# Attention score steps over two units at once and V in plain float32, in a fused scan, attention and expert kernel

## The chip, the cores and the metric

One core of one Trainium2 chip. The metric is the device time of one execution in microseconds; the median of several is compared. The engines are TensorE (PE in the profile; its weight loads PEld), VectorE (DVE), ScalarE (ACT), GpSimd (POOL) and SyncE (SP, which only issues DMAs). Each works through its own list of instructions in order and waits on semaphores.

## What is computed

Eight sequences (batches) of 512 rows by 128, all float32, go through four residual blocks:

```
x = x + scan_block(layernorm(x))
x = x + experts(layernorm(x))
x = x + attention(layernorm(x))
x = x + experts(layernorm(x))
```

The attention has 16 heads of dimension 8 and a local mask: row i sees its own chunk of 10 rows and 25 rows before it.

```
q = (x @ Wq.T + bq) * 8 ** -0.5;  k = x @ Wk.T + bk;  v = x @ Wv.T + bv     # split in 16 heads
out = softmax(q @ k.T + mask) @ v;  out = out @ Wo.T + bo
```

The experts are eight dense feed-forward nets of width 512 (silu(x Wg) * (x Wu), then Wd), each weighed row by row by a product of two softmaxes. The scan block is a gated state space recurrence with 8 states for each of 64 channels.

## The kernel before

**Passes and chunks.** The main work is the experts: two for each batch, 16 passes (ORDER, line 33) of 32 chunks, 512 chunks in all. A chunk c on TensorE is the gate product pg (three float32r products of 512 columns, `split3`, lines 286 to 289), the up product pu of chunk c - 1, and the down products pd of chunk c - 4 (line 1123; 0, 8 or 16 records a chunk, in a pattern of four chunks). A plain float32 product runs as two records. Pass 0 does halves of two batches side by side. ACT turns pg into h by silu (line 1183), DVE multiplies h by pu (line 1232) and every fourth chunk adds the weighed pd to x (line 1220). TensorE may start the gate product of chunk c once silu of c - 2 is done, and the up product of a chunk once the multiplication of the chunk two before is (line 1100).

**Side work.** The scan block (Ssm), the attention (Att) and norm and routing of the coming pass (Head) are woven into the chunks. Each is written as generators, one for each engine, which yield due times in chunks; `interleave` (line 1036) merges them with the main work in order of due time into each engine's list. A due time is only an order: an engine waits for nothing but semaphores, so one that has no main work (POOL, SP) runs ahead. A step with due time s runs in the middle of chunk s, or, if s ends in up to a half, after it. Exp and silu need different tables in ACT, so each exponential among the silus brings a table load before and one after it.

**Attention of batch j** starts at chunk T_ATT[j] = 38 + 55 j (line 65) and must be over by the next expert pass of that batch. TensorE transposes the normed x into a bank (name ln3), ACT copies it as float32r high part axh (line 807), DVE takes the low part axl = x - axh (line 828). Then q and k come by three products each, and V by three products for each of four tiles (lines 750 to 753: 12 products of 128 columns). V goes out to DRAM and comes back in windows as v_w; POOL masks it by heads (like_heads, line 963).

The queries are cut in 17 windows of 30, each with 64 keys. Two windows are a unit (UNITS, 9 a batch, the last with one window), two units a pair (PAIRS, 5 a batch). Scores are made by pairs (scores, line 756; 64 records for a full pair, 16 for the last), into both banks att_ps. The rest runs by units, 512 columns an operation: masks added on DVE (line 897, by halves of 256 columns), row maxima on DVE (maxima, line 845), their subtraction on POOL (line 989), exponential on ACT (line 816), sums and reciprocal on DVE (sums, lines 853 and 854), weighting on POOL (weights, line 974), transpose on DVE into pt (turned, line 863), products with V on TensorE (line 789, 32 records a unit, 16 in the last), and the copy of their result to attT on DVE (dve_out, line 913). Two buffers s_u alternate between units. The step of unit n is due at `Att.at(j, n + S)`, which is T_ATT[j] + 14 + (n + S) * pace, pace 4 chunks, 3.3 in batch 0 and 3.22 in batch 7 (lines 67, 68). The output projection (line 798: four products of 128x128 in plain float32) ends it.

**Scan block of batch i** has its due times in T_SSM (`_ssm_slots`, line 50): st (statistics of x, which SP loads into x_raw, `load_x`, line 1013, due at st - 1 and waiting for the bank of the previous batch's y), rows (norm), ln (transpose), win (input projection, line 409, with a convolution on DVE, lines 542 to 544), dt (product for delta, line 421, and for B and C, line 441), k (four scan steps with POOL and DVE, lines 658 to 718), y (output). These transposes and products share one bank, side_ps, with Head's.

Of the kernel before, what the change touches and what calls it, by code (L numbers as in the profile page):

```python
# [8 lines left out]
F32 = mybir.dt.float32  # L9
# [40 lines left out]
def _ssm_slots(i):  # L50
# [4 lines left out]
    if i == 2:  # L55
        return dict(st=24, rows=25.5, ln=26, win=28.5, dt=32, k=(36, 39, 42, 45), y=50.5)
# [10 lines left out]
S_SC, S_MASK, S_MASK1, S_MAX, S_SUM, S_TURN, S_VAL, S_OUT, S_Q = 1 / 8, 1 / 4, 5 / 8, 3 / 8, 1 / 8, 5 / 8, 7 / 8, 1, 3 / 8  # L67
# [23 lines left out]
def build(nc, x_d, pack_d, wg_d, wu_d, wd_d, out_d):  # L91
    ctx = contextlib.ExitStack()
    with ctx:
# [21 lines left out]
        wv = [sb(f"w_v_{v}", [P, P], F32R) for v in ("hi", "lo")]  # L115
# [42 lines left out]
        att_ar = sb("att_arena", [P, N_S + N_V + L + 8])  # L158
# [12 lines left out]
        rsum = sb("r_sums", [P, 2, 4])  # L171
        smax, = (att_ar[:, o1 + 8 * i:o1 + 8 * i + 8].rearrange("p (w g) -> p w g", w=2) for i in range(1))
# [9 lines left out]
        q_n, k_n = q_room[:, 0, :], k_room[:, 0, :]  # L182

# [37 lines left out]
        x_hi = sem("x_hi")  # L221
# [506 lines left out]
        class Att:  # L728
# [4 lines left out]
            @staticmethod  # L733
            def end(j):
                return Att.at(j, NUNIT + 1)

            @staticmethod
            def pe(pe, link, j):
# [4 lines left out]
                ab.wait_free(pe, ("ln3", j))  # L743
# [28 lines left out]
                yield at(S_SC)  # L772
                ab.wait_free(pe, ("k", j))
                scores(0)
                for n in range(NUNIT):
                    if n % 2 and n + 1 < NUNIT:
                        yield at(n + 1 + S_SC)
                        scores((n + 1) // 2)
                    yield at(n + 1 + S_VAL)
                    if n in (0, NW // 4):  # L780
                        pe.wait_ge(v_set, 4 * j + (4 if n else 2))
                    name = ("o", j, n)
                    ps = ab.take(pe, name)
                    pe.wait_ge(p_t, NUNIT * j + n + 1)

                    for i, w in enumerate(UNITS[n]):
                        for v in range(2):
                            for g in range(4):
                                last = nc.tensor.matmul(ps[32 * g:32 * g + 32, i * QW:(i + 1) * QW],  # L789
                                                        v_w[:, w, v, 32 * g:32 * g + 32], pt[n % 2][:, i, g, v, :],  # L790
                                                        start=(i, v) == (0, 0), stop=(w, v) == (UNITS[n][-1], 1))
# [3 lines left out]
                ab.wait_free(pe, ("o", j, NUNIT - 2))  # L795
                ab.wait_free(pe, ("o", j, NUNIT - 1))
# [6 lines left out]
            def act(act, link, j):  # L803
# [3 lines left out]
                nc.scalar.copy(axh[:, 0:L], ab.ps(("ln3", j))[:, :]).then_inc(x_hi, 1)  # L807
                yield t0 + 6.5
# [3 lines left out]
                for n in range(NUNIT):  # L812
                    yield at(n + 3 / 4)
                    act.wait_ge(s_sub, NUNIT * j + n + 1)
                    u = s_u[n % 2][:, 0:len(UNITS[n]), :, :]
# [3 lines left out]
            def dve(dve, link, j):  # L819
# [7 lines left out]
                dve.wait_ge(x_hi, j + 1)  # L827
                ab.free(nc.vector.tensor_tensor(axl[:, 0:L], ab.ps(("ln3", j))[:, :], axh[:, 0:L].bitcast(F32),
# [540 lines left out]
```

## Time and profile before

| | |
|---|---|
| median of 3 runs | 1431.55 us (1431.43 to 1433.21) |
| the profiled execution | 1431.87 us |
| its span in the profile | 1429.9 us |
| PE busy | 1372.5 us (96%), 12348 records |
| DVE busy | 950.6 us (66%) |
| ACT busy | 769.4 us (54%) |
| POOL busy | 515.7 us (36%) |
| granted clock, mean | 0.991 |

Times in rows are microseconds from the span's start, durations microseconds unless marked ns. A row of the timeline gives start, duration, engine, line, operation, written and read tile, form and count; in square brackets stands the idle time of the engine before it and what ended it. The ends of matmuls are modelled and overlap the next one, so TensorE's work is better read from the distance of two starts. Of a row with "idle before", the number behind the bar is the engine's idle time before such instructions.

### The profile page before, as it was taken

The page shows a single profiled execution, that of the slowest core. Times are in us where ns is not written, and L with a number is a line of the kernel's source. Part 1 is how long each engine was busy: PE and PEld are TensorE (multiplying, and loading weights), DVE is VectorE, ACT ScalarE, POOL GpSimd, SP SyncE. Part 2 cuts the span into 40 slices and gives each one's busy share as a digit, 9 for nine tenths or more (in the row PEclk, how much of TensorE's full clock was granted, in tenths as well). Part 3 has the DMA queues.
Part 4 walks back from the last instruction along what each step waited for, and adds up shares of the span by engine and source line. Part 5 has one row for each costly group of instructions (what it writes and reads, how often), then busy time and mean ns, then how long its engine had stood idle before and what let it go on. Part 6 is the DMA issues. An engine that isn't in the chain of part 4 may idle for free.

```text
span 1429.9 us, 30749 instructions
## 1 busy us (share of the span) xinstructions
PE 1372.5 (96%) x12348; PEld 1193.3 (83%) x12348; DVE 950.6 (66%) x2295; ACT 769.4 (54%) x1041; POOL 515.7 (36%) x517
## 2 busy tenths in 40 slices
PE   4889999999999999999999989999999999999998
PEld 3788878888788888888888878888888888888887
DVE  7665677775876668568675776657856665576543
ACT  6564748553565556637465665456634563365321
POOL 4260654433423453247312751236403421341000
PEclk9899999999999999999999999999999999999999
DMA  7110231003010310121003200050003000300000
GB/s 238 49 36 17 80 66 32 26 6 78 2 47 16 74 21 1 47 67 34 10 1 83 64 1 9 1 116 31 2 1 71 9 2 1 71 9 2 8 1 8
DMA packets 70233, 51.35 MB, mean 36 GB/s; under 512 B 4140, under 2 KB 60508, under 8 KB 70092
## 3 DMA queue, kind: packets, MB, share of 16 engines
q1 hardware_dynamic: 70060, 49.38, 14.2%
q8 instruction: 98, 1.61, 0.5%
q14 instruction: 43, 0.35, 0.1%
q10 hardware_dynamic: 32, 0.02, 0.0%
HBM read 44.92 MB, written 4.46 MB: 35 GB/s over the span
## 4 chain that ended last, share of the span: by engine, by line
PE 79%; DVE 7%; POOL 4%; issue 4%; ACT 3%; DVEq 0%; POOLq 0%
PE pd L1123 26%; PE pg L287 8%; PE pu L287 7%; PE pg L289 7%; PE pg L288 7%; PE pu L288 7%; PE pu L289 7%; PE att_ps L764 2%; POOL arena L709 2%; PE att_ps L789 2%; DVE h L1232 1%; POOL arena L711 1%; DVE x L1220 1%; PE pd L1115 1%; PE side_ps L339 1%
## 5 line engine op out<-in xcount | busy, mean ns | idle before, releaser
L1183 ACT ACTIVATE h<-pg 128x512 f32<-128x512 f32 x512 | 304.3, 598 | 615.9 <-PE pg L289 613.4
L1123 PEld LDWEIGHTS pd<-w_down,h 128*128 128x128 f32 x3840 | 482.6, 192 | 33.3 <-issue 3.5
L1123 PE MATMUL pd<-w_down,h 128*128 128x128 f32 x3840 | 488.8, 275 | 1.1 <-DVE x L1220 1.1
L1232 DVE TENSOR_TENSOR h<-h,pu 128x512 f32<-128x512 f32 x512 | 344.9, 678 | 213.8 <-PE pu L289 203.2
L287 PE MATMUL pg<-ffn_x_hi,w_gate_hi 128*128 128x512 f32 (+1 forms) x544 | 248.1, 456 | 1.1 <-DVE ffn_x_lo L372 1.1
L287 PE MATMUL pu<-ffn_x_hi,w_up_hi 128*128 128x512 f32 (+1 forms) x544 | 210.3, 387 | 10.2 <-DVE h L1232 10.1
L289 PE MATMUL pg<-ffn_x_hi,w_gate_lo 128*128 128x512 f32 (+1 forms) x544 | 208.5, 383 | 0.0
L288 PE MATMUL pg<-ffn_x_lo,w_gate_hi 128*128 128x512 f32 (+1 forms) x544 | 208.5, 383 | 0.0
L288 PE MATMUL pu<-ffn_x_lo,w_up_hi 128*128 128x512 f32 (+1 forms) x544 | 208.5, 383 | 0.0
L289 PE MATMUL pu<-ffn_x_hi,w_up_lo 128*128 128x512 f32 (+1 forms) x544 | 208.2, 383 | 0.0
L974 POOL TENSOR_TENSOR att_arena<-att_arena,r_sums 128x512 f32<-128x512 f32 (+1 forms) x72 | 72.4, 1006 | 273.0 <-DVE r_sums L854 272.9
L1183 ACT ACT_TABLE_LOAD x120 | 154.0, 1283 | 2.1
L1220 DVE SCALAR_TENSOR_TENSOR x<-pd,mix,x 128x128 f32<-128x128 f32 x480 | 134.8, 344 | 18.6 <-PE pd L1123 12.4
L287 PEld LDWEIGHTS pu<-ffn_x_hi,w_up_hi 128*128 128x128 f32 x544 | 102.8, 189 | 37.5 <-DVE h L1232 16.4
L289 PEld LDWEIGHTS pg<-ffn_x_hi,w_gate_lo 128*128 128x128 f32 x544 | 103.5, 190 | 21.7
L289 PEld LDWEIGHTS pu<-ffn_x_hi,w_up_lo 128*128 128x128 f32 x544 | 102.9, 189 | 22.1
L288 PEld LDWEIGHTS pu<-ffn_x_lo,w_up_hi 128*128 128x128 f32 x544 | 103.0, 189 | 21.2
L989 POOL TENSOR_TENSOR att_arena<-att_arena 128x512 f32<-128x512 f32 (+1 forms) x72 | 72.5, 1007 | 132.6 <-DVE att_arena L845 132.0
L287 PEld LDWEIGHTS pg<-ffn_x_hi,w_gate_hi 128*128 128x128 f32 x544 | 104.5, 192 | 13.0 <-issue 2.3
L288 PEld LDWEIGHTS pg<-ffn_x_lo,w_gate_hi 128*128 128x128 f32 x544 | 104.9, 193 | 5.1 <-issue 1.2
L816 ACT ACT_TABLE_LOAD x72 | 92.4, 1283 | 1.3
L709 POOL TENSOR_SCALAR arena<-arena 128x512 f32<-128x512 f32 x28 | 53.9, 1924 | 106.1 <-ACT arena L529 105.3
(226 smaller groups left out, 1512.3 us busy)
## 6 DMA issues: line engine op xcount, KB each, us to landing
arena<-bc_spread SPq DMA_DIRECT2D x56, 256.0 KB, 4.5
att_arena<-v_rows SPq DMA_DIRECT2D x64, 144.0 KB, 3.8
att_arena<-v_rows SPq DMA_DIRECT2D x64, 128.0 KB, 3.7
arena<-in_x SPq DMA_DIRECT2D x8, 256.0 KB, 2.9
x<-in_x SPq DMA_DIRECT2D x8, 256.0 KB, 3.1
w_down<-in_w_down SPq DMA_DIRECT2D x8, 256.0 KB, 4.8
v_rows<-att_arena SPq DMA_DIRECT2D x8, 256.0 KB, 2.3
out<-x SPq DMA_DIRECT2D x8, 256.0 KB, 2.2
```

The source lines that it names most:

```text
L287: nc.tensor.matmul(out, w[0], x_parts[0], start=first, stop=False)
L288: nc.tensor.matmul(out, w[0], x_parts[1], start=False, stop=False)
L289: return nc.tensor.matmul(out, w[1], x_parts[0], start=False, stop=last)
L709: nc.gpsimd.tensor_scalar(d, d, 1e-4, 1.0, ALU.max, ALU.min).then_inc(dec_clip, 1)
L764: last = nc.tensor.matmul(ps[b][64 * c:64 * c + 64, (2 * i + g) * WK:(2 * i + g + 1) * WK], q_w[64 * b:64 * b + 64, m % 2, i, 4 * g + 2 * ...
L816: nc.scalar.activation(u, u, ACT.Exp, scale=float(HD) ** -0.5).then_inc(s_exp, 1)
L974: nc.gpsimd.tensor_tensor(u, u, rsum[:, 0:nw, :].unsqueeze(3).broadcast_to([P, nw, 4, WK]), ALU.mult).then_inc(p_norm, 1)
L989: nc.gpsimd.tensor_tensor(u, u, smax[:, 0:nw, :].unsqueeze(3).broadcast_to([P, nw, 4, WK]), ALU.subtract).then_inc(s_sub, 1)
L1123: last = nc.tensor.matmul(pd[:, t * P:(t + 1) * P], h_b[:, d % NH, t * P:(t + 1) * P], wd[:, d % NCH, :], start=d % CPE == 0 and t == 0, s ...
L1183: nc.scalar.activation(h_b[:, c % NH, :], pg[c % 2][:, :], ACT.Silu).then_inc(gate_done, 1)
L1220: nc.vector.scalar_tensor_tensor(x[:, t, :], pd[:, t * P:(t + 1) * P], mix[m % 2][:, t, e % E:e % E + 1], x[:, t, :], ALU.mult, ALU.add).t ...
L1232: nc.vector.tensor_tensor(h, h, pu[d % 2][:, :], ALU.mult).then_inc(h_done, 1)
```

## The change

Every score step behind the scores themselves runs once for a pair: one buffer of four windows (s_pair) in the place of the two of two windows, 1024 columns an operation; only the masks stay by units. Products with V, their copy-out and the transposes go by pairs too; scores of pair m are now issued before the values of pair m - 1. All due times of these steps change; those of a pair are in units from its start, with the last (one window) scaled by 0.75. V is made by one plain float32 product a tile from a float32 copy of x (axf) that ACT adds, and DVE takes the low part from that copy; wv is a single float32 tile. Batch 2's st, rows, ln, win and dt come 2 to 2.6 chunks later, its k 1.5, its y 1. Waits on the counters are counted in pairs.

```
-        return dict(st=24, rows=25.5, ln=26, win=28.5, dt=32, k=(36, 39, 42, 45), y=50.5)
+        return dict(st=26, rows=27.5, ln=28.6, win=31, dt=34, k=(37.5, 40.5, 43.5, 46.5), y=51.5)
...
-S_SC, S_MASK, S_MASK1, S_MAX, S_SUM, S_TURN, S_VAL, S_OUT, S_Q = 1 / 8, 1 / 4, 5 / 8, 3 / 8, 1 / 8, 5 / 8, 7 / 8, 1, 3 / 8
+S_SC, S_MASK, S_MAX, S_SUB, S_EXP, S_SUM, S_NORM, S_TURN, S_VAL, S_OUT, S_Q = \
+    -0.125, 0.25, 0.5, 0.625, 1.125, 1.375, 1.375, 1.875, 2.75, 2.875, 0.25
+S_LAST = 0.75
...
+            def pair(j, n, part):
+
+                return Att.at(j, n // 2 * 2 + (part if n + 1 < NUNIT else S_LAST * part))
...
+                pe.wait_ge(x_lo, j + 1)
...
                 for t in range(TT):
-                    out, xw = ps[:, t * P:(t + 1) * P], [a[:, t * P:(t + 1) * P] for a in (axh, axl)]
-                    nc.tensor.matmul(out, xw[0], wv[0][:, :], start=True, stop=False)
-                    nc.tensor.matmul(out, xw[1], wv[0][:, :], start=False, stop=False)
-                    last = nc.tensor.matmul(out, xw[0], wv[1][:, :], start=False, stop=True)
+                    last = nc.tensor.matmul(ps[:, t * P:(t + 1) * P], axf[:, t * P:(t + 1) * P], wv[:, :],
+                                            start=True, stop=True)
...
+                def values(m):
+                    pe.wait_ge(v_set, 4 * j + min(m + 1, 4))
...
+                    for i, w in enumerate(PAIRS[m]):
                         for v in range(2):
                             for g in range(4):
                                 last = nc.tensor.matmul(ps[32 * g:32 * g + 32, i * QW:(i + 1) * QW],
+                                                        v_w[:, w, v, 32 * g:32 * g + 32], pt[i // 2][:, i % 2, g, v, :],
+                                                        start=(i, v) == (0, 0), stop=(w, v) == (PAIRS[m][-1], 1))
...
+                for m in range(NPAIR):
+                    yield Att.pair(j, 2 * m, S_SC)
+                    if m == 0:
+                        ab.wait_free(pe, ("k", j))
+                    scores(m)
+                    if m:
+                        yield Att.pair(j, 2 * m - 2, S_VAL)
+                        values(m - 1)
+                yield Att.pair(j, NUNIT - 1, S_VAL)
+                values(NPAIR - 1)
...
+                ab.free(nc.scalar.copy(axf, ab.ps(("ln3", j))[:, :]), ("ln3", j))
...
+                    yield Att.pair(j, 2 * m, S_EXP)
+                    act.wait_ge(s_sub, NPAIR * j + m + 1)
+                    u = att_ar[:, 0:len(PAIRS[m]) * 4 * WK]
                     nc.scalar.activation(u, u, ACT.Exp, scale=float(HD) ** -0.5).then_inc(s_exp, 1)
...
+                ab.wait_free(dve, ("ln3", j))
+                nc.vector.tensor_tensor(axl[:, 0:L], axf, axh[:, 0:L].bitcast(F32), ALU.subtract).then_inc(x_lo, 1)
...
+                for m in range(NPAIR):
+                    yield Att.pair(j, 2 * m, S_MAX)
+                    maxima(m)
+                    yield Att.pair(j, 2 * m, S_SUM)
+                    sums(m)
+                    yield Att.pair(j, 2 * m, S_TURN)
+                    turned(m)
...
-                    yield Att.at(j, n + S_MASK1 - 1 if n % 2 else n + S_MASK)
+                    yield Att.pair(j, n, S_MASK)
                     if n >= 2:
-                        dve.wait_ge(p_t, NUNIT * j + n - 1)
+                        dve.wait_ge(p_t, NPAIR * j + n // 2)
...
+                for m in range(NPAIR):
+                    if m + 1 < NPAIR:
+                        yield Att.pair(j, 2 * m, S_Q)
+                        queries(m + 1)
+                    yield Att.pair(j, 2 * m, S_SUB)
+                    less_maxima(m)
+                    for part in {0: (0, 1), 1: (2, 3)}.get(m, ()):
+                        yield Att.pair(j, 2 * m, 0.9 + part % 2 / 8)
+                        like_heads(part)
+                    yield Att.pair(j, 2 * m, S_NORM)
+                    weights(m)
```

## Rows read from the trace of the kernel before

**Rows 1.** The page: its header, and the chain that ended last, by engine.

```profile
span 1429.9 us, 30749 instructions
...
PE 79%; DVE 7%; POOL 4%; issue 4%; ACT 3%; DVEq 0%; POOLq 0%
```

**Rows 2.** Busy time by stretches: us, PE, PEld, DVE, ACT, POOL, clock, DMA.

```profile
133.70:1323.20 1189.50, 1169.56 (x10995) 1009.86 (x10993) 813.29 (x1954) 667.38 (x882) 463.86 (x462) 1.00 0.14 32
...
1323.20:1429.90 106.70, 101.10 (x632) 89.11 (x630) 46.93 (x114) 28.39 (x47) 1.26 (x2) 0.99 0.02 6
```

**Rows 3.** Timeline of PE, a chunk with nothing beside it: start us, us.

```profile
678.51 0.48 PE L287 MATMUL pg<-ffn_x_hi,w_gate_hi 128*128 128x512 f32 x1
...
680.80 0.48 PE L287 MATMUL pg<-ffn_x_hi,w_gate_hi 128*128 128x512 f32 x1
```

**Rows 4.** Timeline of PE, a chunk with a group of 32 value records.

```profile
832.48 0.48 PE L287 MATMUL pg<-ffn_x_hi,w_gate_hi 128*128 128x512 f32 x1
...
834.95 0.46 PE L789 MATMUL att_ps<-attn_p_t,att_arena 128*32 128x32 f32 x32
...
835.34 0.50 PE L287 MATMUL pg<-ffn_x_hi,w_gate_hi 128*128 128x512 f32 x1
```

**Rows 5.** Timeline of PE, a chunk with the 16 value records of the last unit.

```profile
1048.19 0.48 PE L287 MATMUL pg<-ffn_x_hi,w_gate_hi 128*128 128x512 f32 x1
...
1050.92 0.50 PE L287 MATMUL pg<-ffn_x_hi,w_gate_hi 128*128 128x512 f32 x1
```

**Rows 6.** Timeline of PE, the chunk with V, and one with an output projection.

```profile
621.67 0.48 PE L287 MATMUL pg<-ffn_x_hi,w_gate_hi 128*128 128x512 f32 x1
...
625.34 0.44 PE L287 MATMUL pg<-ffn_x_hi,w_gate_hi 128*128 128x512 f32 x1
...
754.92 0.48 PE L287 MATMUL pg<-ffn_x_hi,w_gate_hi 128*128 128x512 f32 x1
...
758.11 0.48 PE L287 MATMUL pg<-ffn_x_hi,w_gate_hi 128*128 128x512 f32 x1
```

**Rows 7.** Waits of PE: us in total, times, longest us.

```profile
PE pu L287 <- DVE h L1232: 10.1, 11, 1.6
```

**Rows 8.** Groups of instructions by form, whole span.

```profile
L1232 DVE TENSOR_TENSOR h<-h,pu 128x512 f32<-128x512 f32 x512 | 344.9, 678 | 213.8 <-PE pu L289 203.2 <-ACT h L1183 7.2
...
L853 DVE TENSOR_REDUCE r_sums<-att_arena 128x8 f32<-128x512 f32 x64 | 43.4, 678 | 10.6 <-ACT att_arena L816 10.5
...
L853 DVE TENSOR_REDUCE r_sums<-att_arena 128x4 f32<-128x256 f32 x8 | 3.3, 412 | 2.5 <-ACT att_arena L816 2.5
...
L974 POOL TENSOR_TENSOR att_arena<-att_arena,r_sums 128x512 f32<-128x512 f32 x64 | 67.2, 1049 | 232.9 <-DVE r_sums L854 232.8
...
L967 POOL TENSOR_TENSOR att_arena<-att_arena,pack 128x1024 f32<-128x1024 f32 x24 | 45.6, 1912 | 0.0
...
L807 ACT CAST attn_x<-att_ps 128x512 fp32r<-128x512 f32 x8 | 4.7, 583 | 3.3 <-PE att_ps L324 3.3
...
L816 ACT ACTIVATE att_arena<-att_arena 128x256 f32<-128x256 f32 x8 | 3.3, 417 | 0.1
```

**Rows 9.** Timeline of ACT and DVE, an exponential and the sum behind it.

```profile
952.04 1.28 ACT L816 ACT_TABLE_LOAD   x1
...
953.33 0.63 ACT L816 ACTIVATE att_arena<-att_arena 128x512 f32<-128x512 f32 x1
...
954.00 0.69 DVE L853 TENSOR_REDUCE r_sums<-att_arena 128x8 f32<-128x512 f32 x1 [1.11 <-ACT att_arena L816]
```

**Rows 10.** Timeline, batch 2's first steps beside passes 0 and 1.

```profile
112.15 0.87 DVE L303 BATCH_NORM_STATS2 bn_ssm_ln<-arena 128x6 f32<-128x128 f32 x4 [3.33 <-DMA arena<-in_x]
...
124.22 1.12 PE L409 MATMUL side_ps<-arena,pack 128*128 128x512 f32 x2 [1.68 <-DVE ffn_x_lo L372]
...
137.48 0.40 PE L441 MATMUL side_ps<-xs_lo,w_bc_hi 128*16 128x512 f32 x1 [1.63 <-DVE arena L551]
```

**Rows 11.** Line 310, norm rows of DVE: ns min/median/max.

```profile
L310 DVE TENSOR_SCALAR ffn_rows<-x,mv_ffn_ln,rstd_ffn_ln x64: 296/345/2356, 35.2 to 1331.1; 128x128 f32<-128x128 f32 x64
```

More of the change, by code:

```diff
@@ L170, in build @@
         o1 += L
-        rsum = sb("r_sums", [P, 2, 4])
-        smax, = (att_ar[:, o1 + 8 * i:o1 + 8 * i + 8].rearrange("p (w g) -> p w g", w=2) for i in range(1))
+        rsum = sb("r_sums", [P, 4, 4])
+        smax = att_ar[:, o1:o1 + 16].rearrange("p (w g) -> p w g", w=4)
+        s_pair = att_ar[:, 0:2 * L].rearrange("p (w g k) -> p w g k", w=4, g=4)
         xn_att = att_ar[:, 0:L].rearrange("p (t d) -> p t d", t=TT)
@@ L770, in scores @@
                                         ab.fill(last, ("s", j, m, b))
[L772 to L782, printed above, removed]
+                def values(m):
+                    pe.wait_ge(v_set, 4 * j + min(m + 1, 4))
+                    name = ("o", j, m)
                     ps = ab.take(pe, name)
-                    pe.wait_ge(p_t, NUNIT * j + n + 1)
-                    for i, w in enumerate(UNITS[n]):
+                    pe.wait_ge(p_t, NPAIR * j + m + 1)
+                    for i, w in enumerate(PAIRS[m]):
                         for v in range(2):
@@ L866, in dve, with maxima @@
-                for n in range(NUNIT + 1):
-                    if n:
-                        yield at(n + S_SUM)
-                        sums(n - 1)
-                    if n < NUNIT:
-                        yield at(n + S_MAX)
-                        maxima(n)
-                    if n:
-                        yield at(n + S_TURN)
-                        turned(n - 1)
+                def maxima(m):
+                    if 2 * m + 1 < NUNIT:
+                        dve.wait_ge(s_masked, NUNIT // 2 * 2 * j + 2 * m + 2)
+                    ab.wait_free(dve, ("s", j, m, 0))
+                    ab.wait_free(dve, ("s", j, m, 1))
+                    if j or m:
+                        dve.wait_ge(s_sub, NPAIR * j + m)
+                    nw = len(PAIRS[m])
+                    nc.vector.reduce_max(smax[:, 0:nw, :], s_pair[:, 0:nw, :, :], AX).then_inc(s_max, 1)
@@ new lines, in sums, with turned @@
+                def sums(m):
+                    nw = len(PAIRS[m])
+                    dve.wait_ge(s_exp, NPAIR * j + m + 1)
+                    if j or m:
+                        dve.wait_ge(p_norm, NPAIR * j + m)
+                    link(nc.vector.reduce_sum(rsum[:, 0:nw, :], s_pair[:, 0:nw, :, :], AX))
+                    nc.vector.reciprocal(rsum[:, 0:nw, :], rsum[:, 0:nw, :]).then_inc(s_sum, 1)
+                def turned(m):
+                    n = len(PAIRS[m]) * 4 * WK
+                    dve.wait_ge(p_norm, NPAIR * j + m + 1)
+                    if m:
+                        ab.wait(dve, ("o", j, m - 1))
+                    nc.vector.transpose(pt_flat[:, :, :].rearrange("p a l -> p (a l)")[:, 0:n], att_ar[:, 0:n]).then_inc(p_t, 1)
@@ L905, in dve_out @@
             def dve_out(dve, link, j):
-                for n in range(NUNIT):
-                    yield Att.at(j, n + 1 + S_OUT)
-                    nw, name = len(UNITS[n]), ("o", j, n)
-                    nq = WQ if nw == 2 else QW
+                for m in range(NPAIR):
+                    yield Att.pair(j, 2 * m, S_OUT)
+                    nw, name = len(PAIRS[m]), ("o", j, m)
+                    nq = WQ if nw > 1 else QW
                     ab.wait(dve, name)
                     ps = ab.ps(name)[:, 0:nw * QW].rearrange("p (w q) -> p w q", q=QW)[:, :, 0:nq]
-                    to = attT[:, 2 * n * WQ:2 * n * WQ + nw * nq].rearrange("p (w q) -> p w q", q=nq)
+                    to = attT[:, 4 * m * WQ:4 * m * WQ + nw * nq].rearrange("p (w q) -> p w q", q=nq)
                     ab.free(nc.vector.tensor_copy(to, ps), name)
@@ L929, in sp @@
                         if j:
-                            ab.wait(sp, ("o", j - 1, NUNIT - 1))
+                            ab.wait(sp, ("o", j - 1, NPAIR - 1))
                     else:
```

79 lines of the change are left out of this document (18 added, 61 removed).

## The prediction

> **What bounds the kernel now.** I began with the page: its header and the chain that ended last [rows 1]. TensorE is on that chain for 79% of the span, DVE for 7%, POOL for 4%, ACT for 3%. So the time is what TensorE must do plus what it waits for, and the other engines count where they hold it up. Next the busy time by stretches [rows 2]. From the first chunk of pass 1 (133.7 us) to the last attention's output projection (1323.2 us) TensorE is busy for 1169.56 of 1189.50 us and idle for 19.9. Behind that, with no attention left, it idles 5.6 us. The idle that an easier life for DVE, ACT and POOL could give back where this change acts is therefore about 20 us, however much they save; anything beyond has to be TensorE's own work.
>
> A busy matmul in this page overlaps the next, so I price TensorE's work by the timeline: the distance between the gate products of two chunks. With nothing beside the main work and 8 down records a chunk takes 680.80 - 678.51 = 2.29 us [rows 3]. What a chunk holds beyond that is the price of the side group in it. Last, the waits of TensorE [rows 7]: its largest regular one is the up product waiting for h, 10.1 us in 11 waits (0.92 each), which is a late DVE.
>
> **The change, part by part.**
>
> *Products with V.* Nine groups a batch become five: four pairs of 64 records, and the last of 16 as before. A chunk with a group of 32 takes 835.34 - 832.48 = 2.86 us, so the group costs 0.57 [rows 4]. One with the last unit, 16 records, takes 1050.92 - 1048.19 = 2.73, so 0.44 [rows 5]. Sixteen more records thus cost 0.13, and some 0.31 is what TensorE pays to turn to the group and back. A group of 64 should cost 0.57 + 0.26 = 0.83 against 1.14 for two: 0.31 less, 32 times, **-9.9 us**. Bounds: nothing (a group of 64 costs two of 32) and -9.9. I take the upper one, since two sizes of the same group give it.
>
> *V.* Twelve products (three for each tile) become four in plain float32, which run as eight records. The chunk with V takes 625.34 - 621.67 = 3.67, so V costs 1.38. The output projection has just the new form, four 128x128 float32 products as eight records: 758.11 - 754.92 = 3.19, so 0.90 [rows 6]. Saved: 0.48, 8 times, **-3.8 us**. A rule speaks against this part: the Trainium skill, FP8 and Floating Point Precision, TensorE Precision Notes, gives true float32 four passes through the array. Against three products of one pass V would cost a third more, 1.84, and the sum would be 7.5 us higher. This trace disagrees as far as such narrow products go: 0.90 against 1.38.
>
> *Copy of x.* One more ACT copy of 128x512 a batch, like the one at L807 (583 ns, [rows 8]), and DVE's x_lo waits for it. The q products come a chunk after x_lo's slot, over 2 us, and hide it; without that cover it would cost 0.6 a batch, 4.8 in all. I take 0.
>
> *Score steps.* Row maximum, subtraction, exponential, sum, reciprocal, weighting and transpose go from 9 to 5 instructions a batch each. The reduction costs 678 ns at 512 columns and 412 at 256 [rows 8], so 0.15 us fixed; merging saves that much each for maximum, sum and transpose, a little less for reciprocal and copy: about 0.75 us of DVE a pair, 24 in all. POOL at 1024 columns has a row, 1912 ns, against 2 x 1049: 0.19 less, twice a pair [rows 8]. ACT has 32 fewer exponentials and with each up to two table loads of 1.28 us: some 80 us of ACT [rows 9]. None of it is on TensorE's path; it works only through the 20 us of idle. Against it stand lumps: DVE steps of 1.2 us in a row where 0.7 stood, one buffer instead of two, and the sum one chunk after the exponential where it was one and a half. After a table load the 512-wide exponential released DVE's sum 1.96 us after the load began, and DVE had stood for 1.11 [rows 9]. At 1024 columns the exponential is 0.4 longer (0.21 for 256 columns, [rows 8, 9], twice) and the sum 0.5, so the next h comes nearly 1 us later than there. From the end of one up product to the start of the one after the next about two chunks less the product itself pass, well over 3.5 us, for an h of 0.67 [rows 8], so this alone doesn't reach TensorE. In batches 0 and 7 (pace 3.3 and 3.22) rounding puts exponential and sum in the same chunk once each (pair 3, pair 0); there DVE stands for most of 4 us and TensorE may lose 0.5, twice. On the other side the scores come a chunk earlier than the masks now, so masks no longer wait for them, while the copy-out of a pair waits longer for its 64 products. Bounds for the idle: all of it gone (-18, what is left once batch 2's is taken off) and as much again (+18). I take **-2 us**: less load on three engines against bigger lumps.
>
> *Batch 2's first steps.* DVE now sits at slot 24 waiting 3.33 us for x of batch 2 to land [rows 10]. The DMA waits for batch 1's y on TensorE, not for its slot, and nothing stands between slots 23 and 25 in SP's queue, so it starts when it did; at slot 26 it has landed. DVE comes 4.2 us earlier to batch 1's second norm (the wait and 0.87 us of statistics). Then TensorE's wait of 1.68 us before the input projection goes, and most of that of 1.63 before the B and C rows: at the old slot 32 no down products lay between them and the delta product, at slot 34 there are eight. In exchange x_lo of batch 2 has one chunk instead of one and a half after ACT's activations, and the spread of B and C 4 chunks instead of 4.5 before POOL wants it; late next would be the delta product, by up to 0.7 us. Its scans move a chunk and more into batch 0's attention; POOL's last steps of it stand ahead of the first queries, which the first scores (now a chunk earlier) wait for. Bounds -4 and +3; I take **-2.4 us**.
>
> Sum: 9.9 + 3.8 + 2 + 2.4 = 18.1 less. The profiled execution took 1431.87 us (span 1429.9 and 2.0 around it), 0.3 above the median of the runs; so 1413.8, and 1413.5 beside the median.
>
> **The rivals.**
>
> *The idle goes too.* Half the exponentials' table loads are gone and DVE has 24 us less to do; some 11 of the 20 us go instead of 2. For it: TensorE's waits are nearly all for a late DVE. Against it: DVE also waits for POOL and DMAs of the scan, which nothing here shortens. 1431.9 - 13.7 - 2.4 - 11: **1404.5**.
>
> *Merging buys no TensorE time* (the change doesn't do what it says): 64 records cost 1.14. Against it are the two group sizes. **1423.5**.
>
> *POOL's wide steps hold DVE.* A norm step of DVE that takes 345 ns as a rule took up to 2356 beside POOL [rows 11]. Half as many POOL steps, each 1.8 times as long, cover 1.64 times the time in such a collision (the squares of 1.05 and 1.91). I price it at 6 us: **1419.5**. The Trainium skill, VectorE: DVE Perf Modes, where it says what an instruction reads through the second read interface, calls that one shared with GpSimd; the row agrees, and reductions and transposes, with one input each, show no such spread.
>
> *Plain float32 is slow here too*: **1421**, by the rule on four passes; the row of the projection speaks against it.
>
> *Slower: DVE standing for the exponential reaches TensorE.* The place is the sum of each pair, behind the table load and the 1.06 us exponential, with masks, maximum and h queued behind. It decides where DVE meets the sum so early, or ACT is so late, that h misses those 3.5 us and more. If the 11 stalls of 0.92 us become one for each of 32 pairs, that is 29.4 - 10.1 = 19.3 more: 1431.9 - 13.7 - 2.4 + 19.3 = 1435.1, **1434.8** beside the median. It takes 0.58 us a pair to pass the bound. For it: pairs 3 and 0 above; against it: the wait of 1.11 us in rows 9 was followed by none of TensorE.
>
> **How the numbers follow.** About 0.2% (2.9 us) is what a measurement of this kernel can tell from no change, so same is 1428.7 to 1434.4. Forecast 0.46; idle goes too 0.20; no gain by merging 0.10; POOL holds DVE 0.08; slow float32 0.02; DVE's stand 0.14, of it 0.08 past the bound, 0.05 within it and 0.01 short of it. That makes faster 0.87, same 0.05, slower 0.08. The forecast's own range is 1408 to 1419; the range over all runs from 1402, below the case in which the idle goes, to 1426, above merging without gain, and leaves out 2 in 10.
>
> **What would show it.** Right: chunks with 64 value records take about 3.12 us where 8 down records lie beside them; V's chunk 3.19; 40 table loads at the exponential; no DMA wait of DVE near 112 us; idle from pass 1 to the last attention of 16 to 20 us. Wrong: waits of the up product for h well over 10 us, or found after the sums; value groups of 1.1 us; V at 1.8; a new wait of TensorE for queries or for x_lo of batch 2.

## The result and the profile after

The changed kernel takes 1443.89 us, median of 4 runs (1442.41 to 1444.54), against 1431.49 for the kernel before on the same chip (4 runs, 1430.75 to 1433.21). The ratio is 1.0084, 95% interval 1.0069 to 1.0099: it is 12.4 us slower, where I had forecast 18 less. The profiled execution took 1444.54 us, its span is 1442.8. Line numbers of after are those of before plus 5 outside the attention. One execution below, of 4156.68 us in experiment 9, is far outside all others and enters no ratio.

The page of after, its header and the chain that ended last, by engine:

```profile
span 1442.8 us, 30299 instructions
...
PE 75%; DVE 9%; POOL 5%; issue 5%; ACT 4%; DVEq 0%; POOLq 0%
```

TensorE lost four points of the chain against [rows 1]; DVE won two, POOL, ACT and issue one each. The busy time by stretches (us, PE, PEld, DVE, ACT, POOL, clock, DMA share, GB/s), with the same two ends as in [rows 2], the first chunk of pass 1 and the last attention's projection:

```profile
133.20:1336.00 1202.80, 1167.10 (x10959) 1006.40 (x10958) 814.27 (x1797) 602.04 (x809) 455.91 (x398) 0.99 0.14 32
1336.00:1442.80 106.80, 101.17 (x632) 89.17 (x630) 47.01 (x114) 28.44 (x47) 1.27 (x2) 1.00 0.02 6
```

The whole loss is in the first stretch, 1202.80 against 1189.50 us. TensorE idles for 35.7 us in it, where it was 19.9. Its busy time fell only by 2.5 (some 12 of its own work gone, as shown next, and some 10 more spent at a lower clock), and DVE's not at all (814.27 against 813.29), although 157 instructions of DVE are gone. Behind the last attention nothing moved.

**TensorE's own work came out as forecast.** Timeline of PE in after, a chunk with 64 value records and one with V:

```profile
409.62 0.48 PE L292 MATMUL pg<-ffn_x_hi,w_gate_hi 128*128 128x512 f32 x1
...
411.20 0.76 PE L789 MATMUL att_ps<-attn_p_t,att_arena 128*32 128x32 f32 x64
...
412.80 0.48 PE L292 MATMUL pg<-ffn_x_hi,w_gate_hi 128*128 128x512 f32 x1
...
486.21 0.48 PE L292 MATMUL pg<-ffn_x_hi,w_gate_hi 128*128 128x512 f32 x1
...
488.59 1.06 PE L760 MATMUL att_ps<-w_v,q_room 128*128 128x128 f32 x8
...
489.40 0.48 PE L292 MATMUL pg<-ffn_x_hi,w_gate_hi 128*128 128x512 f32 x1
```

Against the quiet chunk of 2.29 or 2.30 us [rows 3], 412.80 - 409.62 = 3.18 makes 0.88 for the group of 64 (0.83 forecast), and 489.40 - 486.21 = 3.19 makes 0.89 for V (0.90 forecast). I took all 479 distances between gate products apart in this way, into a fixed part by the number of down records, the side groups at their usual price, and what is left over, the stall. The side groups fell from 152.1 to 139.8 us, 12.3 less (32 x 0.26 + 8 x 0.49 = 12.2). The stalls rose from 29.8 to 55.7, 25.9 more. Of these, 15.8 are the new idle time. The other 10 fit TensorE's lower clock: the mean granted clock fell from 0.991 to 0.984, and 1.6% of 1442.8 less 0.9% of 1429.9 is 10.2 us, an estimate. So the question is where 26 us of stalls come from.

Why V is cheaper in plain float32 is seen from the starts in before, of float32r products with 512 columns and of V's with 128:

```profile
678.83 0.40 PE L288 MATMUL pg<-ffn_x_lo,w_gate_hi 128*128 128x512 f32 x1
679.06 0.39 PE L289 MATMUL pg<-ffn_x_hi,w_gate_lo 128*128 128x512 f32 x1
...
624.33 0.27 PE L751 MATMUL att_ps<-w_v_hi,attn_x 128*128 128x128 f32 x1
624.45 0.28 PE L752 MATMUL att_ps<-w_v_hi,attn_x 128*128 128x128 f32 x1
```

They are 0.23 and 0.12 us apart (0.115 on the mean of V's twelve, 1.38 / 12). If a pass of 128 columns is a quarter of 0.23, or 0.058 (an estimate), a plain float32 product of V, 0.89 / 4 = 0.22, is about four passes. The Trainium skill (FP8 and Floating Point Precision, TensorE Precision Notes) gives plain float32 four passes, and this trace agrees. It is the narrow float32r product that takes two such passes and not one; why, no run here shows.

Waits of PE and of DVE in after, then those of DVE in before (us in total, times, longest us):

```profile
PE pu L292 <- DVE h L1237: 22.4, 17, 4.0
PE side_ps L329 <- DVE arena L315: 11.9, 5, 7.0
PE side_ps L329 <- DVE ffn_rows L315: 6.6, 5, 4.0
```

```profile
DVE r_sums L863 <- ACT att_arena L828: 33.3, 23, 4.7
...
DVE attn_p_t L872 <- POOL att_arena L979: 12.4, 12, 1.7
```

```profile
DVE att_arena L897 <- PE att_ps L764: 24.8, 20, 2.7
...
DVE r_sums L853 <- ACT att_arena L816: 13.0, 18, 1.8
```

TensorE's wait for h is 22.4 us against 10.1 [rows 7]. That for norm rows (line 315) is 18.5 against 12.0 in before (line 310: 6.9 and 5.1). These two make up the new idle time; smaller waits went. On DVE the wait of the masks for the scores is gone (24.8 before, 1.9 after), as forecast; that of the sum for the exponential went from 13.0 to 33.3, and that of the transpose for POOL's weighting from 3.9, in one wait, to 12.4, in twelve. Three places show how this becomes time. First batch 0's attention in after (timeline of DVE, ACT, POOL and PE; start, length, and in brackets the idle before and its end):

```profile
266.47 0.69 DVE L1237 TENSOR_TENSOR h<-h,pu 128x512 f32<-128x512 f32 x1 [1.38 <-PE pu L294]
...
268.60 1.28 ACT L828 ACT_TABLE_LOAD   x1
...
269.89 1.06 ACT L828 ACTIVATE att_arena<-att_arena 128x1024 f32<-128x1024 f32 x1
...
270.98 1.22 DVE L863 TENSOR_REDUCE r_sums<-att_arena 128x16 f32<-128x1024 f32 x1 [2.56 <-ACT att_arena L828]
...
272.57 2.22 POOL L979 TENSOR_TENSOR att_arena<-att_arena,r_sums 128x1024 f32<-128x1024 f32 x1 [4.03 <-DVE r_sums L864]
273.07 2.80 DVE L664 TENSOR_TENSOR_SCAN arena<-arena 128x512 f32<-128x512 f32 x1
275.79 0.66 DVE L1237 TENSOR_TENSOR h<-h,pu 128x512 f32<-128x512 f32 x1
...
276.50 0.80 PE L292 MATMUL pu<-ffn_x_hi,w_up_hi 128*128 128x512 f32 x1 [3.96 <-DVE h L1237]
```

DVE stands for 2.56 us behind table load and exponential, sums, and then runs the next thing on its list, a scan, beside the weighting that its own sum has just released. The scan takes 2.80 us instead of 1.22. From the end of one h (267.16) to the next (275.79) 8.6 us pass, and the up product waits 3.96. Second, batch 1:

```profile
383.21 1.91 POOL L986 TENSOR_TENSOR att_arena<-att_arena 128x1024 f32<-128x1024 f32 x1
383.41 6.17 DVE L315 TENSOR_SCALAR arena<-arena,mv_ssm_ln,rstd_ssm_ln 128x128 f32<-128x128 f32 x4
...
385.07 4.17 POOL L972 TENSOR_TENSOR att_arena<-att_arena,pack 128x1024 f32<-128x1024 f32 x2
...
389.38 0.58 PE L329 MATMUL side_ps<-pack,arena 128*128 128x128 f32 x2 [1.95 <-DVE arena L315]
...
390.67 0.78 PE L292 MATMUL pg<-ffn_x_hi,w_gate_hi 128*128 128x512 f32 x1
...
391.24 0.63 PE L293 MATMUL pg<-ffn_x_lo,w_gate_hi 128*128 128x512 f32 x1
```

Four norm rows, usually 0.34 us each, take 6.17 us beside three 1024-wide operations of POOL in a row: three of them end within 0.1 us of the ends of the three, the fourth takes 0.33. Only the first of the three is a score step. The other two are masking of V (like_heads), as wide in before; the change issues the last two parts of V right behind one another. TensorE waits, and when it goes on a 512-column product takes 0.63 instead of 0.39. By windows of the same place the granted clock is 1.00 while it works, and 0.69 in the 5.4 us behind the wait, so partly the 1.2 GHz level:

```profile
380.00:386.50 6.50, 6.50 (x102) 5.57 (x101) 6.46 (x14) 1.33 (x3) 4.54 (x4) 1.00 0.01 3
...
390.60:396.00 5.40, 5.40 (x24) 4.50 (x23) 5.25 (x17) 4.71 (x5) 2.43 (x3) 0.69 0.00 0
```

The third place, in batch 4's attention, is like the second, with masking of V alone (timeline of DVE, POOL and PE):

```profile
832.21 4.62 POOL L972 TENSOR_TENSOR att_arena<-att_arena,pack 128x1024 f32<-128x1024 f32 x2
...
832.67 1.98 DVE L663 SCALAR_TENSOR_TENSOR arena<-arena 128x512 f32<-128x512 f32 x1
...
834.68 3.23 DVE L664 TENSOR_TENSOR_SCAN arena<-arena 128x512 f32<-128x512 f32 x1
...
838.54 0.50 PE L292 MATMUL pu<-ffn_x_hi,w_up_hi 128*128 128x512 f32 x1 [2.26 <-DVE h L1237]
```

Of the 22.4 us that TensorE waits for h, 10.4 (six waits) come right behind a scan or the product before it that was held so; behind a sum that had stood come 4.5, in two waits, of which the 3.96 above is in both.

Over the whole timeline, what DVE's norm rows, scans, the products before the scans and the small routing steps take beyond their usual length adds up to about 35 us in before and 56 in after; norm rows alone go from 18.1 to 29.2 (busy for 53.8 and 64.8 us in all). The merged maxima, sums, reciprocals, transposes and copies take 24.4 us less (158.6 to 134.2 for full pairs), so the two nearly cancel: that is why DVE's busy time did not fall. Put down to the POOL step that overlaps each most, 12.6 of the 21 us more lie beside the score steps (9.0 to 21.6), 5.3 beside the masking of V (9.1 to 14.4), whose width did not change, and the rest beside other steps. Which steps are held and which are not is seen in the view by line (ns min/median/max):

```profile
L664 DVE TENSOR_TENSOR_SCAN arena<-arena x28: 1224/1225/3225, 79.7 to 1030.8; 128x512 f32<-128x512 f32 x28
```

```profile
L872 DVE STREAM_TRANSPOSE attn_p_t<-att_arena x40: 432/1236/1247, 214.4 to 1326.5; 128x1024 f32<-128x1024 f32 x32, 128x256 f32<-128x256 f32 x8
```

Transposes never are, nor is the sum's reduction of 1024 columns (at most 1222 ns for a median of 1219), though 15 of the 32 wide transposes and 8 of the 32 wide sums ran for half their time or more beside some POOL operation. Beside a 1024-wide one ran three of these sums and no transpose. The Trainium skill, GPSIMD Engine Reference, Key points, names DVE's instructions in a 2-port mode or with two SBUF inputs as those that contend with GpSimd; this trace agrees in the kinds for a transpose (one input) and a scan (two). A norm row has one such input and is held all the same; by the Trainium skill that takes a 2-port mode, and no row here shows in which mode it runs.

### The profile page after: what moved, and what is told of

It reads as the page before. It is cut to its first block, busy times and chain, and to the rows that moved or that the text cites. A ratio compares the mean times of both kernels' runs of the same rounds, so it can differ in the third digit from the quotient of the medians.

```text
span 1442.8 us, 30299 instructions
## 1 busy us (share of the span) xinstructions
PE 1371.0 (95%) x12316; PEld 1190.6 (83%) x12316; DVE 949.5 (66%) x2134; ACT 703.4 (49%) x968; POOL 507.8 (35%) x453
## 4 chain that ended last, share of the span: by engine, by line
PE 75%; DVE 9%; POOL 5%; issue 5%; ACT 4%; DVEq 0%; POOLq 0%
PE pd L1128 25%; PE pg L292 7%; PE pu L292 7%; PE pg L294 7%; PE pg L293 7%; PE pu L293 7%; PE pu L294 7%; PE att_ps L772 2%; POOL arena L714 2%; PE att_ps L789 1%; DVE h L1237 1%; POOL arena L716 1%; PE pd L1120 1%; DVE arena L663 1%; DVE ffn_rows L315 1%
## 5 line engine op out<-in xcount | busy, mean ns | idle before, releaser
L292 PE MATMUL pu<-ffn_x_hi,w_up_hi 128*128 128x512 f32 (+1 forms) x544 | 211.6, 389 | 22.4 <-DVE h L1237 22.4
L986 POOL TENSOR_TENSOR att_arena<-att_arena 128x1024 f32<-128x1024 f32 (+1 forms) x40 | 66.7, 1668 | 261.4 <-DVE att_arena L855 261.4
L1225 DVE SCALAR_TENSOR_TENSOR x<-pd,mix,x 128x128 f32<-128x128 f32 x480 | 134.7, 343 | 18.5 <-PE pd L1128 12.2
L979 POOL TENSOR_TENSOR att_arena<-att_arena,r_sums 128x1024 f32<-128x1024 f32 (+1 forms) x40 | 66.6, 1665 | 148.7 <-DVE r_sums L864 148.7
L965 POOL TENSOR_TENSOR staged<-q_room,pack 128x256 f32<-128x256 f32 x136 | 84.3, 651 | 20.0 <-ACT q_room L823 20.0
L714 POOL TENSOR_SCALAR arena<-arena 128x512 f32<-128x512 f32 x28 | 53.9, 1925 | 75.9 <-ACT arena L534 75.2
```

Of the source, the lines that this page charges most:

```text
L292: nc.tensor.matmul(out, w[0], x_parts[0], start=first, stop=False)
L714: nc.gpsimd.tensor_scalar(d, d, 1e-4, 1.0, ALU.max, ALU.min).then_inc(dec_clip, 1)
L965: nc.gpsimd.tensor_tensor(q_w[:, m % 2, i, :, :], q, pk("head_q").unsqueeze(2) .broadcast_to([P, 8, QW]), ALU.mult).then_inc(q_set, 1)
L979: nc.gpsimd.tensor_tensor(u, u, rsum[:, 0:nw, :].unsqueeze(3).broadcast_to([P, nw, 4, WK]), ALU.mult).then_inc(p_norm, 1)
L986: nc.gpsimd.tensor_tensor(u, u, smax[:, 0:nw, :].unsqueeze(3).broadcast_to([P, nw, 4, WK]), ALU.subtract).then_inc(s_sub, 1)
L1225: nc.vector.scalar_tensor_tensor(x[:, t, :], pd[:, t * P:(t + 1) * P], mix[m % 2][:, t, e % E:e % E + 1], x[:, t, :], ALU.mult, ALU.add).t ...
```

## The experiments

The theory after this profile: (A) POOL's two score steps, now 1.9 us each and released right in front of DVE's norm rows and scans, hold DVE; (B) the wide exponential makes DVE stand at the sum, and h is late behind it. Rivals: (C) batch 2's later slots move its scans into batch 0's attention; (D) grouping the values makes TensorE itself wait. Ratios are to the kernel before on the same chip.

**1. The change with batch 2's old slots.**

```diff
-        return dict(st=26, rows=27.5, ln=28.6, win=31, dt=34, k=(37.5, 40.5, 43.5, 46.5), y=51.5)
+        return dict(st=24, rows=25.5, ln=26, win=28.5, dt=32, k=(36, 39, 42, 45), y=50.5)
```

> The changed kernel (1443.9 us) with batch 2's slots as they were. Theory C, batch 2's move crowds batch 0's attention: TensorE's stalls in chunks 32 to 92 (24.4 us changed, 9.4 before) fall by 5 to 10 us, the time to about 1436, and the norm rows at chunk 42 no longer fall beside POOL's scan steps. Theories A (POOL's wide steps hold DVE's two-input and norm steps) and B (DVE stands for the wide exponential): the time stays at 1442 to 1446, and chunks 58 and 78 keep stalls of 4 to 5 us.

1444.01 us, ratio 1.0085 (1.0068 to 1.0102). C falls: the move is worth nothing either way inside the change.

**2. The move alone, in the kernel before** (the reverse edit).

> The kernel before with batch 2's first steps two slots further on, and nothing else. My forecast for this part was 2.4 less (bounds 4 less and 3 more); a_shift_back says that it is worth nothing beside the rest of the change. If the waits at 112, 124 and 137 us are given back at once by later ones (x_lo, DVE's norm rows), the time stays within 1 of before; if that giving back came from the wide steps only, it falls by 2 or more here.

1432.02 us, ratio 0.9999 (0.9989 to 1.0009). Also nothing, without any wide step. The waits of [rows 10] do go, and others come within 40 us; timeline of PE with the move alone:

```profile
140.20 0.50 PE L421 MATMUL side_ps<-xs_lo,w_dt_hi 128*128 128x512 f32 x1 [1.25 <-DVE xs_lo L548]
...
148.02 0.50 PE L287 MATMUL pu<-ffn_x_hi,w_up_hi 128*128 128x512 f32 x1 [1.23 <-DVE h L1232]
...
163.06 0.50 PE L287 MATMUL pu<-ffn_x_hi,w_up_hi 128*128 128x512 f32 x1 [2.01 <-DVE h L1232]
```

**3. The change with its exponential a quarter of a unit earlier.** At four chunks a unit that is one chunk earlier in ACT's list, with the sum where it was in DVE's.

```diff
-    -0.125, 0.25, 0.5, 0.625, 1.125, 1.375, 1.375, 1.875, 2.75, 2.875, 0.25
+    -0.125, 0.25, 0.5, 0.625, 0.875, 1.375, 1.375, 1.875, 2.75, 2.875, 0.25
```

> The changed kernel with the exponential due a chunk earlier (S_EXP 0.875 for 1.125), so that the sum comes two chunks behind it. Theory B: DVE's wait for the exponential falls from 33.3 us to under 12, the stalls of the up product for h from 22.4 to about 12, the time to 1433 to 1437. Theory A: DVE's wait falls too, but the time stays within 3 us of 1443.9, because the long norm rows and scans stay.

1437.26 us, ratio 1.0035 (1.0024 to 1.0046): some 7 us of the loss are gone. The sum's wait fell from 33.3 to 7.8 us, but the wait for h hardly (20.6 from 22.4). Waits of DVE in this run:

```profile
DVE attn_p_t L872 <- POOL att_arena L979: 10.4, 10, 1.7
DVE r_sums L863 <- ACT att_arena L828: 7.8, 6, 2.6
```

Over the whole span of this profile, its fastest execution (1433.66 us, clock 0.990), TensorE is idle for 3.9 us less than in after (67.9 for 71.8) and busy for 7.0 less with the same 12316 records (1364.0 for 1371.0), so most of what came back is the clock. B is true and is worth 7 us; it isn't the whole, and little of it shows as a shorter wait for h.

**4. The change with POOL's subtraction and weighting in halves of 512 columns,** everything else as it is; waits for them count both halves.

```diff
-                    u = s_pair[:, 0:nw, :, :]
                     pool.wait_ge(s_sum, NPAIR * j + m + 1)
-                    nc.gpsimd.tensor_tensor(u, u, rsum[:, 0:nw, :].unsqueeze(3).broadcast_to([P, nw, 4, WK]),
-                                            ALU.mult).then_inc(p_norm, 1)
+                    for a in range(0, nw, 2):
+                        z = min(a + 2, nw)
+                        u = s_pair[:, a:z, :, :]
+                        nc.gpsimd.tensor_tensor(u, u, rsum[:, a:z, :].unsqueeze(3).broadcast_to([P, z - a, 4, WK]),
+                                                ALU.mult).then_inc(p_norm, 1)
...
```

> The changed kernel with POOL's two steps of a pair each in two instructions of 512 columns; all else, DVE's and ACT's 1024 columns too, as in the change. POOL has 12 us more to do. Theory A: norm rows and scans of DVE held by a POOL instruction are held half as long each, 6 to 12 us of stalls go, the time is 1432 to 1438. Theory B: POOL's result comes 0.2 us later, the time is 1444 to 1447.

1433.94 us, ratio 1.0008 (0.9992 to 1.0024), the runs from 1429.47 to 1437.33 and the profiled one the longest. Some 10 us come back by the medians (6.6 to 14.4 by single runs) with POOL's work larger (519.6 us busy for 507.8), so the width has a price of its own. But theory A's account of it fails: it had the held times halved, and norm rows are held for 25.9 us, from 29.2, scans no less. Two halves in a row cover the same time. The products before the scans are busy for 24.2 us, from 27.7, and the wait for h is 20.3. TensorE idles 3.5 us less over the whole span even in this slowest execution.

**5 and 6. The change, and the kernel before, with POOL's two steps on 1 of 64 key columns.** These leave out the subtraction of the maximum and the weighting for the other 63; instructions, order and waits stay.

```diff
+                    u = u[:, :, :, 0:1]
-                    nc.gpsimd.tensor_tensor(u, u, rsum[:, 0:nw, :].unsqueeze(3).broadcast_to([P, nw, 4, WK]),
-                                            ALU.mult).then_inc(p_norm, 1)
+                    nc.gpsimd.tensor_tensor(u, u, rsum[:, 0:nw, :].unsqueeze(3), ALU.mult).then_inc(p_norm, 1)
...
```

> The changed kernel with POOL's subtraction and weighting cut to one key column of 64, so the maxima and the sums are applied to that column alone; waits, order and everything else stay. Beside b_pool_tiny. Theory A, in the form that the first runs leave of it (POOL's steps of the scores, wider or not, now fall on DVE's norm rows and scans and on its wait for the transpose): the held time of the norm rows falls from about 30 us to under 15, the time to 1426 to 1430, and the distance to b_pool_tiny is -3 us or better, where changed and before are +12 apart. Theory B (the stand for the exponential alone): 1438 or more, still 6 us or more above b_pool_tiny.

> The kernel before with the same cut of POOL's subtraction and weighting. Both theories: little, 1425 to 1431, since POOL's 512-wide steps hold the norm rows for only 13 us in all there.

The change drops to 1419.82 us, ratio 0.9921 (0.9906 to 0.9936); the kernel before to 1427.89, 0.9976 (0.9967 to 0.9986). So the two steps cost 1.0084 - 0.9921 = 1.6%, 23 us, in the change and 0.24%, 3.4 us, before. Without them the change is 8 us the faster. That is more than theory A had (1426 to 1430), though the excess of norm rows fell less than it had: to 18.3 us, not under 15. In the kernel before it is 14.5, from 18.1 and not from the 13 of the expectation. This is the largest single cause. It bundles what POOL's steps hold on DVE, what they delay POOL's other steps, and the wait of the transpose for them (12.4 us in after, in no row any more here). No run parts these cleanly; in experiment 4 the last wait rose to 15.6 us while the time fell by 10, which speaks against it as the main part. Waits of DVE in the change without POOL's steps:

```profile
DVE r_sums L863 <- ACT att_arena L828: 37.1, 25, 4.7
```

The sum waits for the exponential as much as ever. Whether that still costs anything is the next question.

**7. The same with the exponential early as well.**

> Leaves out, as a_pool_tiny does, the subtraction of the maximum and the weighting for 63 of 64 key columns, and sets the exponential a quarter of a unit earlier besides. If the wait of DVE's sum for the exponential (37.1 us in a_pool_tiny) is a loss of its own that POOL's steps only cover, as half of the theory has it, the time falls by a further 4 to 6, to about 1415, and TensorE's waits for h from 15 to 10 or less. If the exponential's stand costs TensorE only where POOL's steps have made DVE late already (the rival, for which it speaks that the two mends overlapped with POOL's split: 10 and 7 gave 12), the wait of the sum shrinks to under 10 us as in a_exp_early and the time stays within 1.5 of 1419.8.

1412.76 us, ratio 0.9861 (0.9846 to 0.9875): 7 us below experiment 5 by the medians, 9 by the ratios, which were taken on two chips. The theory holds against its rival: the stand at the sum costs some 7 us with POOL's steps whole and without them. Windows of this run, the first stretch, and its waits of PE and DVE:

```profile
133.20:1304.00 1170.80, 1152.91 (x10954) 997.07 (x10953) 790.02 (x1796) 597.47 (x805) 341.01 (x398) 1.00 0.15 33
```

```profile
PE pu L292 <- DVE h L1237: 12.4, 13, 2.0
```

```profile
DVE r_sums L863 <- ACT att_arena L828: 6.7, 5, 2.6
```

TensorE idles for 17.9 us, the waits for h are back near the 10.1 of before. DVE's busy time is 23.3 below before's 813.29, and the merged steps' own rows give 24.6 (158.6 to 134.0 us): the 24 us of fixed costs that I had worked out. The excess on the held steps is about 31 us, against 35. With both causes away the change lies 15.1 us under the kernel before with the same cut (1427.89). Of that, 12.2 are TensorE's own work. The rest isn't idle time: over the whole span TensorE is idle for 53.9 us here and 54.2 there. The mean clock of the two profiles, 0.994 and 0.991, can account for it.

**8. Both mends with the computation whole:** halves on POOL and the early exponential.

> The changed kernel with both mends: POOL's steps in two halves and the exponential a chunk earlier. Alone they gave 10 and 7 us. If they act on different stalls: 1426 to 1430. If both only make the same chain shorter: 1432 to 1436.

1432.05 us, ratio 0.9996 (0.9985 to 1.0007). 7 and 10 gave 12 together, the second of the two outcomes named: beside the halves the early exponential is worth only 2 us (experiment 4 against this one). So its 7 us are no fixed price. Mended so, the change only breaks even.

**9. V in plain float32 alone, in the kernel before.**

```diff
-                    out, xw = ps[:, t * P:(t + 1) * P], [a[:, t * P:(t + 1) * P] for a in (axh, axl)]
-                    nc.tensor.matmul(out, xw[0], wv[0][:, :], start=True, stop=False)
-                    nc.tensor.matmul(out, xw[1], wv[0][:, :], start=False, stop=False)
-                    last = nc.tensor.matmul(out, xw[0], wv[1][:, :], start=False, stop=True)
+                    last = nc.tensor.matmul(ps[:, t * P:(t + 1) * P], axf[:, t * P:(t + 1) * P], wv[:, :],
+                                            start=True, stop=True)
...
+                ab.free(nc.scalar.copy(axf, ab.ps(("ln3", j))[:, :]), ("ln3", j))
```

> The kernel before with V in plain float32 alone (one more ACT copy of 128x512 a batch, eight records in place of twelve). The chunk accounting gives V 0.49 us less a batch: if that is all, 3.9 less, 1427.6, and b_v32_valpairs (1426.5) then owes only 1.1 to its value pairs. If the added copy and the later x_lo hold something up, the time stays within 1.5 of before, and the value pairs brought nearly all of the 5.

1430.41 us, ratio 0.9983 (0.9974 to 0.9992): 2.4 less, 1.1 to 3.7 by the interval, so most of the 3.9 and not surely all. No row of its profile is read.

**10. V and the value pairs, in the kernel before:** values and their copy-out by pairs, every score step by single units as it was.

```diff
-                    name = ("o", j, n)
+                    m = n // 2
+                    if m in (0, 2):
+                        pe.wait_ge(v_set, 4 * j + (4 if m else 2))
+                    name = ("o", j, m)
...
-                    for i, w in enumerate(UNITS[n]):
+                    for i, w in enumerate(PAIRS[m]):
```

> The kernel before with V in plain float32 and the products with V and their copy-out by pairs; score steps stay by units of 512 columns, batch 2 as before. If TensorE's savings are real and the loss lies in the wide score steps and batch 2's move: 3.8 us for V and 8 to 10 for 32 merged groups, 1418 to 1421 us, with stalls of 28 to 33 us in passes 1 to 15 as before. If later products and copy-outs are what hurts: 1428 or more.

1426.52 us, ratio 0.9961 (0.9946 to 0.9975), between the two outcomes named. It is the fastest kernel here that leaves nothing out, and faster than both before and after. The value pairs bring some 3 of their 8.3 beyond V. The 479 distances add up to 4.9 us less than in before and the side groups to 12.2 less, so its stalls are some 37 us against 29.8. One of them is new and its own, in the timeline of PE: the pair's product waits for the masks, which DVE does first:

```profile
847.31 0.76 PE L790 MATMUL att_ps<-attn_p_t,att_arena 128*32 128x32 f32 x64 [2.66 <-DVE att_arena L898]
```

**11. The same with values and copy-out one chunk later,** to take that wait away.

```diff
-                    yield at(n + 1 + S_VAL)
+                    yield at(n + 1 + S_VAL + 1 / 4)
...
-                    yield Att.at(j, n + 1 + S_OUT)
+                    yield Att.at(j, min(2 * m + 2, NUNIT) + S_OUT + 1 / 4)
```

> b_v32_valpairs (1426.5 us) with products with V and copy-out of a pair one chunk later. There TensorE waited 2.66 us at one group for the masks to free its bank, and half-clock chunks followed. If that wait is what is missing of the 12 us that merging and V should give: 1421 to 1424. If the longer groups simply meet other late steps of DVE: 1425 to 1428.

1427.51 us, ratio 0.9974 (0.9961 to 0.9986): no better. That wait is gone, and 4 us behind its place, at 851.40, TensorE waits 2.86 us for h. D is true for some 5 of the 8.3 us that grouping saves, but not by that one wait. Why they go I have not settled. One lead is in the rows: DVE's wait of the sum for the exponential is 13.0 us in before, 23.6 in experiment 10 and 32.1 here, with 512-wide steps.

## Why the prediction was wrong

- **TensorE's own work: right.** 9.9 + 3.8 forecast, 8.3 + 3.9 measured by the same distances. The group of 64 costs 0.88, not 0.83; V 0.49 less, not 0.48. The price of V came from the right row, but the reading that the trace disagrees with the Trainium skill on four passes was wrong: as the rows at 624.33 show, what takes longer than it was priced at is the three-product form.
- **The copy of x: nearly right.** Experiment 9 leaves at most 2.8 us for it.
- **Batch 2's move: wrong.** I took -2.4; it is 0, inside the change and alone. The interval of the move alone is 1.6 less to 1.3 more. The three waits I counted do go. The step that failed is that I priced waits as if the chain behind them were free: within 40 us TensorE waits 1.25 us for the delta product's input and 1.23 and 2.01 for h. I named the first as "late next, by up to 0.7" and left it out of the sum.
- **Score steps: this step failed.** "I take -2 us: less load on three engines against bigger lumps" measured +26: stalls of 55.7 us for 29.8, outside my bound of +18. The saved load is real (24 us of DVE) and was eaten up on DVE itself, where steps held beside POOL take 21 us longer. What the runs showed in place of the -2 is two losses: POOL's two score steps, some 20 us more than before, and DVE's stand at the exponential, 7.
- **The slack of 3.5 us: failed.** I compared an exponential 0.4 and a sum 0.5 longer with the room for h as if they stood alone. In the row at 270.98 the stand is 2.56, and the scan behind it is held for 1.6 more. Loss: 7 us in experiments 3 and 7, but only 2 beside POOL's halves. The rival on DVE's stand, at 19.3, had the right engine and nearly three times the price; of the one stall a pair that it named, two in 32 are found.
- **POOL's wide steps hold DVE: right in kind, at less than a third of its price.** I gave 6 us; it is some 20 (23 in the change less 3.4 before), with what the bundle of experiment 5 holds besides. The square of the length (1.65; I wrote 1.64) scales collisions that are there already: it would make the 9.0 us held beside score steps 15, and they are 21.6. It leaves out that steps fall elsewhere: the subtraction at 383.21 in front of two masking steps of V made a row of 6 us of POOL against which the norm rows ran. And it leaves out TensorE's lower clock, 10 us in all.
- **The cases were taken as alternatives.** Each rival alone stayed near or under the kernel before. Two of them came true together, on the same engine, and no case of mine held that. So the chance for slower was 0.08.
- **Signals.** 38 table loads at the exponential (40 forecast), no DMA wait at 112 us, 3.18 and 3.19 for the two chunks: as said. Idle is 35.7 for 16 to 20. Waits for h are 22.4, well over 10, which I had named as making the forecast wrong; that they would be found after the sums holds for 4.5 us of them.

By the experiments the 12.4 us are: the change without its two harms -15 (experiment 7 against 6), DVE's stand at the exponential +7 (5 against 7), POOL's longer steps on DVE and its transposes +20 (23 less 3.4). These differences add up to the result by construction; what stands apart from them is experiment 3, which gives the 7 again with POOL's steps whole, and the distances between gate products, which give 12.2 of the 15. Experiment 8 shows that the two harms overlap, so another order of taking them away could part them otherwise.

## What to carry to other kernels

Merging two instructions saves their fixed cost, but where another engine waits in a list written by hand, price the lump: what stands behind it in each engine's list, and what runs beside it. A long POOL operation beside DVE's two-input or norm steps held those here until it ended (norm rows of 1.8 to 2.4 us for 0.34, a scan of 3.2 for 1.22), so put such DVE steps where POOL is idle, or keep POOL's short and apart: in halves right behind one another they held nearly as much. Take merges apart: here the values by pairs with V in plain float32 win 0.4%, and the whole change, with the score steps by pairs, is 0.8% slower than before.

## What the runs showed of the hardware that I had not expected

- Four norm rows of DVE (128x128, one SBUF input and two scalars per partition) can take 6.17 us instead of 1.4 beside three POOL operations of 128x1024, and a scan of 128x512 3.2 instead of 1.22. Reductions and transposes of 128x1024 took at most 12 ns over their medians, beside POOL's work or not.
- More idle time of TensorE came with a further loss through its clock: 15.8 us more idle went with some 10 us more by the lower mean clock. Two places show the order, a granted clock of 1.00 up to a wait and 0.69 and 0.70 behind it (390.60 in after; 847.30 in experiment 10, behind the wait of 2.66 us). Executions of one kernel differ by the clock too: four of the ten of experiment 4 took 1429.5 to 1430.2 us with a mean clock of 0.993, three 1437.2 to 1437.3 with 0.986. What made these differ no run shows.
- A float32r product of 128x128 by 128 columns took 0.11 to 0.12 us from start to start and one of 512 columns 0.23, so the narrow one costs twice as much a column; a plain float32 product of 128 columns took 0.22.
